# Attend steps in pairs: two 256-column halves of PSUM banks `ops`, and new orders for five engines

## The reference, cut to what matters

```python
xn = _layernorm(x)
# attention: windows of KS = 4 rows at a step of ST = 2, 8 heads of 64
qkv = xn @ w_qkv                                   # 512 -> 1536
win = qkv[:, idx]                                  # (B, N, 4, 1536)
dots = einsum('bnqhd,bnkhd->bnhqk', q, k) * scale
o = einsum('bnhqk,bnkhd->bnqhd', softmax(dots), v)
y = o @ w_out + b_out
out = zeros.at[:, idx.reshape(-1), :].add(y)       # windows overlap by half
# feed-forward, every operand through fp4_quant_dequant
h = silu(xq @ wgate_q.T) * (xq @ wup_q.T)          # 512 -> 1408
return x + out + hq @ wdown_q.T                    # 1408 -> 512
```

## Time and profile before

| what | us |
|---|---|
| median of 3 runs (lowest, highest) | 2214.14 (2213.77, 2217.5) |
| the profiled execution: its own time | 2211.99 |
| its span in the trace | 2209.8 |
| attention stage (until the first matmul of the feed-forward) | 836.3 |
| feed-forward stage (the rest) | 1373.5 |
| PE busy, whole span | 2152.9 (97%) |
| DVE busy, ACT busy, POOL busy | 1663.1, 657.1, 1219.6 |

### The profile page before, as it was taken

The page is one execution under the profiler, slowest core; times in us unless marked ns, Lnnn a source line. Parts: engine busy times, 40 slices in busy tenths (PEclk is TensorE's granted clock), DMA queues, the critical chain, the costliest instruction groups (busy, mean ns, idle before and its releaser), DMA issues.

```text
span 2209.8 us, 46872 instructions
## 1 busy us (share of the span) xinstructions
PE 2152.9 (97%) x16712; PEld 1045.1 (47%) x16712; DVE 1663.1 (75%) x3108; ACT 657.1 (30%) x1009; POOL 1219.6 (55%) x877
## 2 busy tenths in 40 slices
PE   4999999999999989999999999999999999999999
PEld 1445454544545444444444444444444444444444
DVE  7777878778687665778778777787787877878774
ACT  3233333333343322222222222222222232222221
POOL 3266767676675544555555555555555555555553
PEclk9999999999999999999999999999999999999999
DMA  9656666585756444333333433333334333343333
GB/s 270 175 124 177 156 148 180 125 198 127 181 151 167 131 137 129 78 90 80 87 83 79 94 75 85 89 81 87 83 77 91 78 87 84 77 92 76 87 74 68
DMA packets 449418, 251.82 MB, mean 114 GB/s; under 512 B 367282, under 2 KB 373938, under 8 KB 449300
## 3 DMA queue, kind: packets, MB, share of 16 engines
q1 hardware_dynamic: 448404, 246.99, 46.0%
q10 hardware_dynamic: 576, 2.10, 0.2%
q0 software_dynamic: 320, 0.97, 0.2%
HBM read 99.01 MB, written 59.77 MB: 72 GB/s over the span
## 4 chain that ended last, share of the span: by engine, by line
PE 89%; DVE 4%; issue 3%; DMA 1%; SPq 1%; POOL 1%; ACT 0%; DVEq 0%; POOLq 0%; ACTq 0%
PE acc L977 19%; PE prj L1345 7%; PE ops L1345 7%; PE prj L977 6%; PE acc L1326 5%; PE acc L1330 5%; PE acc L1327 5%; PE prj L1347 3%; PE ops L1347 3%; PE acc L1328 2%; PE sps L1328 2%; PE sps L1331 2%; PE acc L1331 2%; PE sps L1329 2%; PE acc L1329 2%
## 5 line engine op out<-in xcount | busy, mean ns | idle before, releaser
L977 PE MATMUL acc<-late 128*128 128x512 f16 x2304 | 518.8, 382 | 15.0 <-DMA late<-xh 10.4
L977 PEld LDWEIGHTS acc<-late 128*128 128x128 f16 x2304 | 220.9, 98 | 281.8 <-issue 21.2
L208 POOL TENSOR_TENSOR qk<-qk,xh 128x1408 f32<-128x1408 f32 x64 | 165.7, 2590 | 230.0 <-DVE qk L245 230.0
L1220 DVE SCALAR_TENSOR_TENSOR qk<-acc,row_gains,xh 128x512 f32<-128x512 f32 x64 | 48.0, 751 | 260.4 <-ACT xh L1285 260.4
L203 POOL TENSOR_TENSOR qk<-qk,xh 128x1024 f32<-128x1024 f32 (+1 forms) x128 | 177.5, 1387 | 111.1 <-DVE xh L224 111.1
L213 POOL TENSOR_TENSOR v<-qk,v 128x1408 f16<-128x1408 f32 x64 | 183.1, 2860 | 100.3 <-ACT v L255 100.3
L1345 PE MATMUL prj<-late,qk 128*128 128x512 f16 x704 | 214.6, 379 | 0.7 <-DMA qk<-v 0.7
L1345 PE MATMUL ops<-late,qk 128*128 128x512 f16 x704 | 214.6, 379 | 0.0
L255 ACT ACTIVATE v<-qk 128x1408 f16<-128x1408 f32 x64 | 88.1, 1377 | 367.4 <-POOL qk L208 367.4
L1326 PE MATMUL acc<-late,turned 128*128 128x512 f16 x512 | 194.0, 379 | 0.4 <-DVE qk L1220 0.4
L1330 PE MATMUL acc<-late,turned 128*128 128x512 f16 x512 | 194.0, 379 | 0.0
(11 more groups left out here) (158 smaller groups left out, 4440.8 us busy)
## 6 DMA issues: line engine op xcount, KB each, us to landing
normed<-late SPq DMA_DIRECT2D x64, 256.0 KB, 2.7
res<-in_L_attn_x SPq DMA_DIRECT2D x64, 256.0 KB, 3.1
attended<-res SPq DMA_DIRECT2D x64, 256.0 KB, 2.6
raw<-normed SPq DMA_DIRECT2D x64, 256.0 KB, 2.7
v<-attended SPq DMA_DIRECT2D x64, 256.0 KB, 2.7
out<-v SPq DMA_DIRECT2D x64, 256.0 KB, 2.0
late<-in_L_attn_x SPq DMA_DIRECT2D x62, 256.0 KB, 3.9
ready<-turned SPq DMA_DIRECT2D x36, 256.0 KB, 2.3
```

The costliest lines, as they stand in the source:

```text
L208: pool.tensor_tensor(blocks(v), blocks(v), spread(s[3]), ALU.mult).then_inc(q["valued"], 1)
L977: last = pe.matmul(out, lhsT, rhs, start=(at == 0), stop=(at == n - 1))
```

## The change

In PSUM, `attend` now writes step a into one of two halves of the two `ops` banks, 256 columns each: the first step of a pair into columns 0 to 255, the second into 256 to 511. `PAIRS` gives first and last step of each one's pair: (0,1), (2,3), 4 alone, (5,6), (7,8). PE waits for ACT's copy of the step before only ahead of the first of a pair. ACT's copy of either half waits until the last step of the pair is done (`pv_done`). There are still nine copies a batch, one for each half; no copy is merged with another. The matmuls, their number and their shapes are as before. Behind the attention, the second `first_rounder` of ACT gets a wait of its own for `rounded`.

```diff
+PAIRS = [(0, 1), (0, 1), (2, 3), (2, 3), (4, 4), (5, 6), (5, 6), (7, 8), (7, 8)]
...
         def attended(b, a):
-            act.wait_ge(pv_done, at(b, ATT, a))
-            src = ops[:, :, 0:2 * P].rearrange("p g (c q) -> p c g q", c=KC)
+            act.wait_ge(pv_done, at(b, ATT, PAIRS[a][1]))
+            src = ops[:, :, (a - PAIRS[a][0]) * 2 * P:(a - PAIRS[a][0] + 1) * 2 * P].rearrange("p g (c q) -> p c g q", c=KC)
...
         def first_rounder(b, k):
+            if k == 1:
+                act.wait_ge(rows.q["rounded"], 1)
             rounder(act, rows.q, rows.raw[:, k, :], rows.rounder, k)
...
         def attend(b, a):
+            half = (a - PAIRS[a][0]) * 2 * P
...
-            pe.wait_ge(o_out, at(b, ATT, a - 1))
+            if a == PAIRS[a][0]:
+                pe.wait_ge(o_out, at(b, ATT, a - 1))
...
-                    last = pe.matmul(ops[DH * (h % 2):DH * (h % 2) + DH, g, h // 2 * DH:(h // 2 + 1) * DH],
+                    last = pe.matmul(ops[DH * (h % 2):DH * (h % 2) + DH, g,
+                                         half + h // 2 * DH:half + (h // 2 + 1) * DH],
...
         batches(pe,
-                "p6' v4 s1 a0 v5 a1 p7' v6 s2 v7 a2 q0+ q1+ q2+ a3 q3+ q4+ q5+ a4 q6+ q7+",
-                "v0+ p0 a5 v1+ s0+ p1 a6 v2+ p2 a7 v3+ q8+ q9+ q10+ q11+ p3 q12+ q13+ p4 a8 q14+ p5 q15+",
+                "p6' v4 s1 v5 p7' a0 a1 v6 s2 v7 q0+ q1+ q2+ a2 a3 q3+ q4+ q5+ a4 q6+ q7+",
+                "v0+ p0 v1+ s0+ p1 a5 a6 v2+ p2 v3+ q8+ q9+ q10+ q11+ p3 q12+ q13+ a7 a8 p4 q14+ p5 q15+",
```

All four strings of all five engines are new. In the loop, each engine has the same steps as before, in another order. The strings of the second half for DVE, POOL and SP, and ACT's, which the prediction follows:

```diff
-  DVE  "A0 k2 w4 n5+ R0 n6+ d0 d1 A1 u2 z2 w5 A2 R1 d2 f0 n7+ w6 w7 m0+ d3 f1 c0+ A3 d4 k0+ R2 A4 d5 f2 R3 g0+ A5 f3 d6 w8"
+  DVE  "A0 n5+ w4 R0 k2 A1 d0 n6+ d1 d2 A2 R1 n7+ u2 R2 d3 f0 z2 w5 w6 f1 f2 A3 m0+ R3 A4 A5 c0+ k0+ d4 w7 w8 g0+ d5 f3 d6"
-  POOL "b1 w3 w4 r1+ b2 V0 w5 l4+ X0 l5+ O0 o0 V1 o1 w6 V2 l6+ w7 X1 O1 o2 l7+ V3 b3 X2 ..."
+  POOL "b1 r1+ w3 w4 w5 l4+ V0 X0 l5+ O0 V1 o0 V2 X1 O1 o1 l6+ w6 b2 o2 l7+ X2 w7 O2 o3 b3 w8 ..."
-  ACT  "q0+ q1+ o2 q2+ q3+ o3 x4+ B0 x5+ q4+ o4 H0 q5+ e2 h0 B1 h1 x6+ q6+ q7+ h2 B2 v0+ o5 ..."
+  ACT  "q0+ q1+ x4+ q2+ q3+ o2 B0 o3 x5+ q4+ q5+ o4 H0 q6+ e2 h0 B1 B2 q7+ H1 x6+ x7+ h1 h2 v0+ o5 ..."
-  SP   "L0 k2+ r2 e6 L1 e7 k3+ L2 T0 S0 r3 s0 L3 t4+ t5+ t6+ T1 L4 t7+ r4 S1 s1 s2 T2"
+  SP   "L0 e6 e7 k2+ L1 L2 t4+ k3+ T0 r2 r3 S0 t5+ L3 L4 T1 t6+ t7+ S1 s0 s1 T2 r4 s2"
```

## The result

The changed kernel takes 2225.88 us (median of 6 runs, 2221.02 to 2228.58); the kernel before, on the same chip, 2213.38 (6 runs). The ratio is 1.0058, with a 95% interval of 1.0044 to 1.0072: slower by 0.6%, where 2205.6 was forecast and 2219 was the top of the range. The profiled span went from 2209.8 to 2225.1 us, 15.3 more.

A forecast was written before the change was run, and what follows sets the result against it. PE, busy 97%, was taken to bound the kernel. Pairs -6.5, transposes -4.2, new wait +7.2, head -3, tail -2 sum to -8.5: 2212.0 - 8.5 + 2.1 = 2205.6 us, 8-in-10 range 2197 to 2219.

The forecast's parts named there:

- What bounds the kernel: Whole kernel: PE, busy 97% of the span; all of the effect lies in the first 836 us.
- Pairs, -6.5: Attends side by side in loop and tail: the second costs 0.49 us, not 0.73; 27 x 0.24 = -6.5 us.
- The transposes, -4.2: Loop, PE's wait at `q8` for turned rows held back in SP's queue: 0.7 a batch should go, -4.2 us.
- The wait at (5,6), +7.2: Loop, PE waits at pair (5,6) for DVE's late turn for `a6`: 1.2 us a pass, +7.2 (0 to 14.4).
- the other pairs have room: Loop: no wait at the other pairs; DVE turns for `a2`, `a3` right after `z1`, three blocks before PE comes.
- Head -3: Head: the 2.17 us stall inside `a2`, read as a late packet, and the slow clock behind it go: -3 us.
- tail -2: Tail: the 1.81 us stall inside `a2` goes, though `p1` may move later: -2 us (-4 to +3.7).
- a stall of over 2 us with a low clock where there was none: One of the listed signs in PE's timeline that would show the forecast wrong.
- The rival of the stalls that stay: Head and tail give nothing: -3.7, 2210.4 us; 0.25 together with the eaten gain, within the borders.
- The rule of the Trainium skill that I weighed there: Crossing a 16 KB block costs a mostly hidden step; head gives nothing, tail only 0.2: -3.7, 2210.4 us.
- POOL's spread for `a6`, my slower case: Loop: a POOL step delays the turn for `a6`, wait 3.65 a pass, 2220.3 us; slower in all had 0.15.
- a wait that I don't see in five new orders: Unnamed wait, place and size not given, counted with POOL's order in the 0.15 for slower.

The follow-up runs named there:

- a_v2first: Changed kernel with DVE's `z1` ahead of `m2` and `n4`, TensorE's `v2` ahead of `s0`, `v3` behind `p2`, 6 repeated calls in the head's `a4`: 2199.28 us, 0.9939.
- a_pad60: Changed kernel with 60 increments of two unused semaphores on TensorE's queue before its first matmul: 2211.89 us, ratio 1.0005.
- a_z1: Changed kernel with DVE's loop order alone changed, `z1` ahead of `m2` and `n4`, `n4` behind `w3`: 2218.0 us, ratio 1.0020.
- b_a5late: Kernel before with, on TensorE alone, the loop's `a5` moved behind `p1`, directly ahead of `a6`, without a pair: 2234.68 us, ratio 1.0113.
- a_256: Changed kernel with 64 repeated calls (256 instructions, one whole packet) more in the head's `a4`: 2220.91 us, ratio 1.0046.
- b_a0late: Kernel before with, on TensorE alone, the loop's `a0` moved behind `p7`, directly ahead of `a1`, without a pair: 2230.45 us, ratio 1.0068.

## Why the prediction was wrong, point by point

**What bounds the kernel: right.** All 15 us are on PE, in the attention stage, and nearly all of them in the six passes.

**Pairs, -6.5: right.** 64 records take 1.18 us in one piece, and the next block starts 1.11 behind the pair's start (549.33 to 550.44), where it starts 0.63 behind a single one (539.41 to 540.04 in the kernel before): 0.48 for the second, against my 0.49. In the changed kernel `ops` is 3.7 us less busy in the six passes, with one attend more; a_v2first, where the four pairs a pass have no idle at all, has 4.9 less. The 0.48 leaves no room for a drain between attends of the same tile shape, as the Trainium skill has it in "TensorEngine Tiling (Array Packing)", section Key Properties.

**The transposes, -4.2: right.** The idle ahead of `acc` in the six passes went from 3.9 to 0.

**The wait at (5,6), +7.2: wrong in place, two thirds of the size.** There is none there, and not in a_pad60 either, where no stall of `s0` gives DVE time. It came at (2,3), in five passes of six: 3.8 us of idle, and 4.9 from the start of `a2` to the block behind `a3`, since a pair that is torn apart also loses what it saved. I had written there that "the other pairs have room", because DVE turns for them right after `z1`. I had not followed what stands ahead of `z1`: `m2` and `n4`, 2.9 us of DVE in one pass (512.10 to 514.98), with POOL's spreads behind `z1`. The early `z1` of a_z1 took it away.

**Head -3: not decided by the time; tail -2: wrong.** `s0` of the first pass starts at 142.3 where it started at 142.8, so the head as a whole gave 0.5. But its first projections began 2.2 us later (33.34 in place of 31.13, both behind a DMA), and this place moves from run to run: b_a5late has the head of the kernel before, and its `s0` starts at 139.3. The stall of 2.17 in `a2` and the slow clock behind it are gone (36 matmuls in 7.93 us, not 9.57), as forecast, though b_a5late with the old head also shows 7.94; a new stall of 1.1 us cut `s2` behind its 85th record, where both attends of the pair now stand ahead. From `s1` to `s0` the head is 3.8 us shorter (46.4 to 42.6), 0.6 of it the `a5` that now stands behind `s0`. The tail, from `s0` behind the last pass to the end of the attention stage, went from 105.7 to 106.6: the stall in `a2` is gone, and `s0`, whole before, is cut for 1.7 us.

**The step that failed** is a term put at nothing: late packets in the loop. I priced them in the head and the tail alone, by the count of instructions from the old stall: "At the same count of instructions PE is now 19 matmuls into `q0`, `q1`, 4 us later, since `a2` has moved away: the packet should be there." I had the right mechanism, a late packet behind dense small records, and used it only at the two places where the kernel before showed a stall. I did not ask where packets end in the loop, though I had `a5` moved past `s0` in my own list of edits. What I wrote as a sign of being wrong, "a stall of over 2 us with a low clock where there was none", is what came. The sum had no term for a stall that the kernel before did not show. Measured in the six passes it is +16.8 us of idle and +9.6 for the slow clock behind it. Against that stands a gain that it did not have either, -6.1 in busy `sps`. The forecast terms as measured, with the pairs at 24 times 0.25, give about -6.0 - 3.9 + 4.9 - 0.5 + 0.9 = -4.6, and these three +20.3: +15.7, where the span has +15.3.

**The rivals.** The rival of the stalls that stay came nearest: stalls did stay in head and tail, though not in their old places. It had none in the loop. The rule of the Trainium skill that I weighed there ("Runtime: NRT & Kernel Launch", section Instruction fetch mechanics: crossing a block is mostly hidden) holds here by count and not by cost: to 70 packets in the six passes there are seven stands, but each of the seven costs 2 to 3 us, behind dense small matmuls. POOL's spread for `a6`, my slower case, did not occur; slower had 0.15, in part for "a wait that I don't see in five new orders". Something unseen did come, but it was no wait for another engine: no rival named what made the kernel slower.

## What to carry to other kernels

Where an engine issues small instructions faster than its program can be loaded, any edit that moves instructions past such a stretch is an edit of where the packets end: count the instructions moved and look at every dense stretch behind them. A change judged on its time alone can be refused or kept for a reason that has nothing to do with it: this one is 0.6% slower as written and 0.6% faster with two fp16 blocks and two DVE steps in another place. The sign of the accident is a stall named "issue" behind the same record of the same block in every pass; if sixty idle instructions ahead of the loop move it, data, other engines and the order of the steps are out.

## What the runs showed of the hardware that I had not expected

- Sixty instructions that do nothing for the result, issued before the first matmul, are worth -12 us in one kernel and +24 in the other.
- The stall has a period of 256 instructions in the code (60 and 320 more act alike, 256 more act as none) and doesn't depend on how many were issued before.
- In the loop a block of 384 instructions, all of them dense, runs without a stop when the border lies 2, 8 or 20 behind its start or at 158 and above, stands up to 0.9 us at 32, and 1.1 to 3.6 at 44 to 102. At 138 the loss comes behind the block. Single passes don't keep to this: `s1` at 244 stood 1.1 to 2.6 us at its 122nd record in one pass of six in most kernels that had the border there (in two of a_256). Nor is the edge the same everywhere: in the tail `s0` was cut behind record 142 in the changed kernel (1.7 us) and 130 in a_v2first (1.3 us), which are borders at 28 and 4. That `s1` with a border at 20 was cut, for 1.0 to 1.9 us, and `s0` was not, is open: what the fetch had to do in the blocks ahead of them differs.
- Behind an idle of 2 to 3 us the granted clock fell to 0.5 to 0.6 for about 4 us in most passes but not in all (in one pass of the changed kernel `p1` behind it ran at 1.00): 9.6 us on top of 16.8. It isn't special to packets: in b_a0late `p1` took 4.3 to 4.4 us behind three waits of 1.9 us for DVE.
- Short of a stall, dense blocks can run slower by gaps of 0.1 to 0.3 us about every half microsecond, 1 us a block, at full clock. The changed kernel has 6.1 us less of them in the loop. The cause is open.
